# First layer's windowed attention: the loop over batches written out in one block

## The reference, cut to what matters

```python
def _L0_attn_ref(x, wq, wk, wv, wo, q_norm_w, k_norm_w):
    H, HD = (16, 64)
    WINDOW = 64
    ...
    q = rmsnorm(x @ wq.T, q_norm_w)
    k = rmsnorm(x @ wk.T, k_norm_w)
    v = x @ wv.T
    ...
    scores = jnp.einsum('bhqd,bhkd->bhqk', q, k) * scale
    scores = scores + slopes[:, None, None] * dist[None, :, :]
    causal = (dist > 0) | (dist < -WINDOW)
    scores = jnp.where(causal[None, None], neg_inf, scores)
    weights = jax.nn.softmax(scores, axis=-1)
    out = jnp.einsum('bhqk,bhkd->bhqd', weights, v)
    ...
    return out @ wo.T

h = _layernorm(x, axis=-1) * (1 + ca) + sa
x = x + ga * _L0_attn_ref(h, L0_attn_wq, ...)
```

## Time and profile before

| | us |
|---|---|
| median of 3 runs (2198.72 to 2205.35) | 2204.37 |
| the profiled execution, its own time | 2193.19 |
| its span in the profile | 2191.1 |
| the touched stage in it, first matmul to last residual add | 102.4 to 650.9 |
| one head pair in the steady part of it | 15.84 |

### The profile page before, as it was taken

The page is one execution under the profiler, slowest core; times in us unless marked ns, Lnnn a source line. Parts: engine busy times, 40 slices in busy tenths (PEclk is TensorE's granted clock), DMA queues, the critical chain, the costliest instruction groups (busy, mean ns, idle before and its releaser), DMA issues. The chain is left out here.

```text
span 2191.1 us, 34634 instructions
## 1 busy us (share of the span) xinstructions
PE 1609.8 (73%) x11536; PEld 932.3 (43%) x11536; DVE 1342.9 (61%) x3346; ACT 1139.5 (52%) x2956; POOL 564.4 (26%) x613
## 2 busy tenths in 40 slices
PE   6899898998983169923799999999999822421930
PEld 4378676786763159922122222222222322421920
DVE  5555454554558322237799999999999277540523
ACT  3076665765652024424288888888888631210310
POOL 3122222222225740066100100100100021374046
PEclk9799999999995579966599999999999956655965
DMA  4811010111100157624100000000000000012832
GB/s 144 311 37 37 20 38 21 37 30 28 38 21 22 50 183 233 193 58 128 59 18 24 25 22 19 25 24 17 24 25 3 1 2 0 4 47 84 255 107 74
DMA packets 85871, 136.51 MB, mean 62 GB/s; under 512 B 17872, under 2 KB 57040, under 8 KB 85552
## 3 DMA queue, kind: packets, MB, share of 16 engines
q1 hardware_dynamic: 62704, 89.43, 14.2%
q0 software_dynamic: 11744, 34.49, 4.8%
q10 hardware_dynamic: 11232, 10.23, 1.4%
HBM read 72.89 MB, written 45.09 MB: 54 GB/s over the span
## 5 line engine op out<-in xcount | busy, mean ns | idle before, releaser
L1822 DVE TENSOR_REDUCE q_max<-s_ps 128x1 f32<-128x1024 f32 x512 | 597.8, 1218 | 14.8 <-PE s_ps L1713 7.3
L1803 ACT ACTIVATE probs<-s_ps 128x512 f32<-128x512 f32 x1024 | 535.6, 603 | 124.7 <-PE s_ps L1734 124.4
L1713 PE MATMUL s_ps<-k_stack,q_stack 64*128 64x512 bf16 x1024 | 351.1, 397 | 17.0 <-PEq L94 8.3
L1734 PE MATMUL s_ps<-q_stack,k_stack 64*128 64x512 bf16 x1024 | 319.7, 384 | 20.1 <-ACT probs L1803 15.4
L1748 PE MATMUL o_ps<-probs,v_aug 128*32 128x512 f32 x2048 | 273.6, 606 | 0.7 <-ACT probs L1803 0.7
L876 POOL TENSOR_TENSOR probs<-probs,p_rsum 128x512 f32<-128x512 f32 x128 | 133.1, 1040 | 373.0 <-DVE p_rsum L855 373.0
L811 ACT ACTIVATE probs<-s_biased,s_min 128x128 f32<-128x128 f32 x512 | 199.5, 395 | 44.8 <-DVE s_min L849 44.8
L1734 PEld LDWEIGHTS s_ps<-q_stack,k_stack 64*128 64x128 bf16 x1024 | 78.5, 94 | 334.1 <-ACT probs L1803 281.9
L849 DVE CUSTOM_DVE_ANT_0 s_biased<-score_ps,nbias 128x128 f32<-128x128 f32 x512 | 117.6, 286 | 70.5 <-PE score_ps L737 69.6
L737 PE MATMUL score_ps<-k_pad,q_bd 128*128 128x128 f32 x1024 | 144.2, 284 | 0.0
L833 DVE TENSOR_SCALAR q_bd<-proj_ps,qscale 64x512 f32<-64x512 f32 x64 | 48.4, 756 | 137.0 <-PE proj_ps L715 134.1
(11 more groups left out here) (296 smaller groups left out, 2799.2 us busy)
## 6 DMA issues: line engine op xcount, KB each, us to landing
moe0b_wblock<-in_L_ffn_blocks SPq DMA_DIRECT2D x39, 578.0 KB, 4.3
moe_rows<-zero_rows POOLq DMA_DIRECT2D x6, 2880.0 KB, 28.2
moe1b_wblock<-in_L_ffn_blocks SPq DMA_DIRECT2D x39, 256.0 KB, 3.7
v_shift<-v_tiles SPq DMA_DIRECT2D x32, 256.0 KB, 3.1
v_shift<-v_tiles SPq DMA_DIRECT2D x32, 224.0 KB, 3.6
qk_parts_dram<-qk_parts SPq DMA_DIRECT2D x16, 384.0 KB, 2.7
q_stack<-qk_parts_dram SPq DMA_DIRECT2D x192, 32.0 KB
k_stack<-qk_parts_dram SPq DMA_DIRECT2D x192, 32.0 KB
```

The lines of the kernel that those rows point to most:

```text
L1713: mm = nc.tensor.matmul(s1[u % 2][:, c * CH:(c + 1) * CH], qs[head_rows(m), quad % 4, j, qt * P:(qt + 1) * P], ks[head_rows(m), quad % 4, ...
L1734: nc.tensor.matmul(bank_of("exp", 4 * k + pos)[:], ks[head_rows(m), quad % 4, j, kt * P:(kt + 1) * P], qs[head_rows(m), quad % 4, j, half ...
L1803: nc.scalar.activation(pr[:, k % 2, HEADS[pos], :], bank_of("exp", n)[:], ACT.Exp).then_inc(sm["exp"], 1)
L1822: v.tensor_reduce(mx[:, h % 4, col:col + 1], s1[u % 2][:], AX.X, ALU.max).then_inc(sm["maxed"], 1)
```

## The change

The hardware loop goes. All 32 head pairs of the four batches (`HP = B * PAIRS`) are numbered through in one block, and the pipeline runs on from pair 7 of a batch to pair 0 of the next: the projections of the next batch's first pair stand in the steps of the last pair. The barrier and the clearing between batches go with the loop, semaphores count through to the end, and addresses are constants.

What stood once in a batch is placed inside the stream: ACT copies the next batch's tokens in step 4 of the batch before, into one of two halves of `nat`; the residual add of a batch stands in DVE's step 5 of the next batch; POOL makes the next gated weights in step 5, between its products of groups 4 and 5, and before it waits until the last output projection of the old batch is done. TensorE's first output projection of a batch (step 7) waits for both the new weights (`wo_gated`) and the two adds that empty the banks (`x_added`, new).

```diff
-        hb = K.nat[:, 0:TPB, :].rearrange("p t d -> p (t d)")
+        hb = [K.nat[:, i * TPB:(i + 1) * TPB, :].rearrange("p t d -> p (t d)") for i in range(2)]
...
-        G = PAIRS * GRP
-        units = [(h, u) for h in range(PAIRS) for u in range(6)]
+        HP = B * PAIRS
+        G = HP * GRP
+        units = [(h, u) for h in range(HP) for u in range(6)]
...
             h = g // GRP + 1
-            if h >= PAIRS or g >= G:
+            if h >= HP or g >= G:
                 return []
             return [6 * h + u for u in ((0, 1), (2, 3), (4,), (5,))[g % GRP]]
 
-        with nc.Fori(0, B) as b:
-            with nc.Block() as block:
+        with nc.Block() as block:
...
+                    b, hw = divmod(h, PAIRS)
+                    tok = slice(b * T + half * CH, b * T + (half + 1) * CH)
...
+                        bb, hw = divmod(hh, PAIRS)
+                        if hw == 0:
+                            pe.wait_ge(wo_gated, bb + 1)
+                            if bb >= 1:
+                                pe.wait_ge(x_added, 2 * bb)
...
+                def copy_tokens(b):
+
+                    if b >= 2:
+                        act.wait_ge(a_out, 6 * PAIRS * (b - 1))
+                    nc.scalar.copy(hb[b % 2], K.hT[:, b * T:(b + 1) * T]).then_inc(h_in, 1)
...
+                for g in range(G + 3):
+                    for n in unit_steps(g):
                         evacuate(n)
...
+                    if g % (GRP * PAIRS) == GRP and g // (GRP * PAIRS) + 1 < B:
+                        copy_tokens(g // (GRP * PAIRS) + 1)
...
+                def residual(b):
+
+                    dve.wait_ge(wo_mm, PAIRS * (b + 1))
+                    for i in range(2):
+                        xs = K.x[:, b * TPB + i * CPT:b * TPB + (i + 1) * CPT, :]
+                        v.tensor_tensor(xs, xs, wp[i][:], ALU.add).then_inc(x_added, 1)
+
+                for g in range(G + 2):
+                    if g > GRP * PAIRS and g % (GRP * PAIRS) == GRP + 1:
+                        residual(g // (GRP * PAIRS) - 1)
...
+                residual(B - 1)
...
+                for g in range(G):
+                    if g == 0 or g > GRP * PAIRS and g % (GRP * PAIRS) == GRP + 1:
+                        b = g // (GRP * PAIRS)
+                        if b >= 1:
+                            pool.wait_ge(wo_mm, PAIRS * b)
+                        nc.gpsimd.tensor_tensor(wog[:], wo[:], bc(K.mod_rows[:, 0, b, GA, :], 1, PAIRS), ALU.mult
+                                                ).then_inc(wo_gated, 1)
+                    pool.wait_ge(rsum, g + 1)
...
-                    sp.wait_ge(v_sh0, 16 * PAIRS)
-                    sp.wait_ge(v_sh1, 16 * PAIRS)
-            nc.all_engine_barrier(sems_to_clear=clear)
-        with nc.Block() as block:
...
+                sp.wait_ge(v_sh0, 16 * HP)
+                sp.wait_ge(v_sh1, 16 * HP)
                 sp.wait_ge(cleared, 16 * (ROWS // P // ZR // 9))
```

More of the change, by code:

```diff
@@ L684, in window_attention_stage @@
         wp = [K.ps(f"wo_ps{i}", [P, CPT, D], st) for i in range(2)]
-        ((h_in, p_mm, a_out, q_out, v_sh0, v_sh1, s_mm, biased, exped, rsum, normed, turned, pt_out, pv_mm, o_out,
-          wo_mm, wo_gated), clear) = K.win_sems
+        (h_in, p_mm, a_out, q_out, v_sh0, v_sh1, s_mm, biased, exped, rsum, normed, turned, pt_out, pv_mm, o_out,
+         wo_mm, wo_gated, x_added) = K.sems(
+            st, "win", "h_in", "proj_mm", "act_out", "q_out", "v_shift_even", "v_shift_odd", "score_mm", "biased",
+            "exp", "rsum", "normed", "turned", "probsT_out", "pv_mm", "o_out", "wo_mm", "wo_gated", "x_added")
@@ L891, in _ @@
             @block.sync
             def _(sp):
+                for h in range(HP):
+                    sp.wait_ge(a_out, 6 * h + 6)
+                    if h >= 2:
+                        sp.wait_ge(pv_mm, GRP * (h - 1))
+                    sp.dma_start(vs[BLK:P, h % 2], vv[0:BLK, h % 2]).then_inc(v_sh[h % 2], 16)
+                    sp.dma_start(vs[0:BLK, h % 2, 1:TPB], vv[BLK:P, h % 2, 0:TPB - 1]).then_inc(v_sh[h % 2], 16)
+                sp.wait_ge(v_sh0, 16 * HP)
+                sp.wait_ge(v_sh1, 16 * HP)
@@ L2115, in build @@
         K = Core(nc, ctx)
-        K.win_sems = K.loop_sems(
-            "win", "h_in", "proj_mm", "act_out", "q_out", "v_shift_even", "v_shift_odd", "score_mm", "biased", "exp",
-            "rsum", "normed", "turned", "probsT_out", "pv_mm", "o_out", "wo_mm", "wo_gated")
         K.x = K.sb("x", [P, NT, D])
```

320 lines of the change are left out of this document (150 added, 170 removed).

## The result

The changed kernel takes 0.9828 of the time of before, with a 95% interval of 0.9808 to 0.9848: 2164.7 us against 2203.5 us, medians of three and four executions. Two later comparisons gave 0.985 (0.9829 to 0.987) and 0.9827 (0.9804 to 0.985). By the medians of the three comparisons it is faster by 33 to 39 us, where 33.7 was predicted (2170, in a range of 2157 to 2185). A fourth execution of the changed kernel in the first comparison took 2885.5 us at a mean granted clock of 0.545; it is left out of these numbers, none of the ten later executions was like it, and whether the change has a part in it stays open.

The account below looks back on a forecast made before the run. TensorE was taken to bound the steady part (busy 15.64 of 15.84 us a pair), with idle time at batch borders. Savings of 34.3 less 0.6 us, 33.7 off the median 2204.4, gave 2170.7, rounded to 2170 us; range 2157 to 2185.

Parts of the forecast that it names:

- The border sum: Three batch borders: three-pair windows of 58.96, 59.34 and 58.62 us each fall to the steady 47.53, saving 34.3 us.
- What a border consists of: Border 1's 11.4 us: 2.8 from lower clock, 8.6 idle PE, of which 5.11 between adds and first projection.
- The placed work: Token copy, residual add and gated weights inside the running pipeline: mostly covered, cost 0.2 us a border, 0.6 in all.
- the cover of POOL's product of group 5: Time between that product's end, behind the placed weights, and PE needing it: 0.3 us, which two handovers may use up.
- Rival one: At the borders the copy, adds and weights delay the chain by their full length: 14.0 us cost, 2184 us; chance 0.07.
- rival two: Steady pairs also get faster, as run-time addresses or the sequencer cost PE 0.2 us a pair: 2163.5 us; chance 0.05.
- Rival three: Hidden instruction transfers of the long stream stall PE 3.8 us once a pair: 122 us lost, 2292 us; chance 0.03.
- Rival four: Granted clock falls to 0.94 over about 515 us without pause, costing 32 us: 2202 us, no change; chance 0.03.
- The end of the stage: Last add to the next stage's first instruction: 1.79 us before, taken as the same, bounds -1.8 and +1.8.
- From the profile to the median: 33.7 us off the profiled 2193.19 gives 2159.5; the median before lies 11.2 us higher, so 2170 was predicted.

Follow-up runs that it names:

- the drained kernel: Changed kernel, no loop or barrier, but every engine's stream drains at a batch's end and restarts with six lone projections; ratio to before 0.9879, 2175.1 us.

## Why the prediction was right, step by step

**The border sum.** Predicted 34.3 us, found 34.3 us in the same windows. Comparing like stretches by a mark that comes once a pair was enough; it took no knowledge of what a border consists of. The sum also holds for the reason given: the windows after have the same 463 matmul records (464 in one), at the steady pace and a clock of 1.00.

**What a border consists of.** The prediction put 2.8 us of border 1 down to the clock and 8.6 to idle time, and read 5.11 us as the gap, with POOL's early return as the sign of code being fetched. The runs bear out that the branch makes the gap: without it the gap is 0.80 us, with it and no run-time addresses 4.81. That the gap is the fetching of code stays argued. The 2.8 us are not all the clock: in the drained kernel, with a clock of 1.00 in the whole window, PE's records are still 48.15 us against 46.92, so 1.2 us of the 2.8 stays at full clock and 1.6 goes with the slow one. The total is untouched by this split. The largest single part of the saving is the branch, 14 of 34 us; the drain that the new numbering removes is 10.8.

**The placed work.** Predicted 0.2 us a border, found 0.01 to 0.02. The mis-sized term is the cover of POOL's product of group 5: 0.3 us predicted, 0.77 us read from the profile after (the product ends at 258.92, the transposes start at 259.69), and 0.95 with TensorE's own slack, measured by doubling the weights. The prediction moved everything behind the add by its full 1.28 us. In the profile of after, set off by the 46.05 us between the marks of the two pairs (198.96 and 245.01), the add starts at 252.27, just where the bias stood (206.22 + 46.05), but the reciprocal comes at 254.31 instead of 253.41, 0.9 us late: part of the delay fell into the 0.21 us that the reciprocal had waited for ACT anyway, and the records of neighbouring instructions overlap a little. The weights start before the product's record ends (255.56 and 255.60), too.

```profile
252.27 1.27 DVE L860 TENSOR_TENSOR x<-x,wo_ps 128x512 f32<-128x512 f32 x2
...
253.46 0.28 DVE L874 CUSTOM_DVE_ANT_0 s_biased<-score_ps,nbias 128x128 f32<-128x128 f32 x1
...
254.56 1.04 POOL L901 TENSOR_TENSOR probs<-probs,p_rsum 128x512 f32<-128x512 f32 x1 [1.66 <-DVE p_rsum L880]
...
255.56 2.36 POOL L897 TENSOR_TENSOR woT_gated<-woT,mod_rows 128x1024 f32<-128x1024 f32 x1
...
257.88 1.04 POOL L901 TENSOR_TENSOR probs<-probs,p_rsum 128x512 f32<-128x512 f32 x1
...
259.69 0.60 PE L751 MATMUL probsT_ps<-ident,probs 128*128 128x128 f32 x4
```

Rival one (none of it covered) is out; that it could bite is shown by the doubled weights. The price of late weights shows in the pair behind the window (17.26 us with the doubled weights), and not in pair 1 of the later batches, where the prediction says to look for rival one.

**The steady part, rivals two to four.** The pairs take 15.846 us, against 15.844 before; rival two (a faster steady part) is out, and the run with constant addresses inside the loop says the same. Rival three (instruction transfers that starve TensorE) is out by the same number. Rival four (the clock does not hold) is out for the executions compared: the clock is 1.00 from 109.55 to 613.70 in the profile after.

**The end of the stage.** Taken as equal within 1.8 us, found 0.08 us shorter.

**From the profile to the median.** Predicted 2170 for 2165 measured. For the profiled execution the sum gave 2159.5 and 2164.4 was measured, 4.9 us more: the first profile of before was the quick one without the stall at the end, so the two first profiles lie only 28.8 us apart. The sum was taken off the median of before although its durations came from an execution 11 us quicker; that was sound, as the second profile of before shows the same borders in a span 8.2 us longer. What the first comparison gives beyond 34.3 us, some 3.6 us by its ratio, lies within its interval: 34.3 of 2203.5 us is a ratio of 0.9844, inside 0.9808 to 0.9848, as it is inside the intervals of the two later comparisons. No part of it was traced to the change.

## What to carry to other kernels

Cut the trace by an event that comes once in a unit of work, and compare stretches with the same units inside and across a border: the difference is the whole price of the border, ready to be summed. When a hardware loop has few and long passes, write it out before rearranging anything; here that alone gave 14 of the 34 us, and the numbering through gave the rest. Work placed in a running pipeline is free up to a cover that can be measured by doubling it; here the doubled work cost its length less 0.95 us. Look for its cost where TensorE takes up the result, which can lie behind the stretch in which the work stands.

## What the runs showed of the hardware

A barrier over all engines that also clears 17 semaphores left TensorE only 0.80 us idle between the last add and the next matmul (the run with a block per batch); a branch back to the head of a long body made it 4.5 to 5.1 us (the kernel before and the loop with constants). POOL, whose stream is much shorter than TensorE's, was back after 1.17 us (its weights start at 237.15, the add ends at 235.98, in the loop with constants).

The last stage's DVE stood 2.4 to 3.1 us between two of its own instructions in ten of the eleven profiles, with a releaser that the profile does not name. Why the first profile of before is without it stays open.
